# Two batches of attention prepared, and the first batch's maxima taken, among the expert loads before it

## The reference

```python
x = x + 0.5 * ffn(layernorm(x), gate_w, expert_bias, w1, w2, w3)
x = x + attention(layernorm(x), Wq, Wk, Wv, Wo)
x = x + 0.5 * ffn(layernorm(x), gate_w, expert_bias, w1, w2, w3)
```

## Time and profile before

| | us |
|---|---|
| median of 3 runs | 844.98 |
| the three runs | 844.72, 844.98, 851.7 |
| the profiled execution | 854.1 |
| its span, first to last instruction | 852.3 |

### The profile page before, as it was taken

One profiled execution on the slowest core, in us unless ns is written; L12 is line 12 of the kernel. 1 busy time (PEld: TensorE's weight loads), 2 busy tenths in 40 slices (PEclk: granted clock), 3 DMA queues, 4 the chain that ended last, 5 costly groups with the idle time before them and its releaser, 6 DMA issues.

```text
span 852.3 us, 14693 instructions
## 1 busy us (share of the span) xinstructions
PE 651.6 (76%) x4966; PEld 483.1 (57%) x4966; DVE 437.5 (51%) x1115; ACT 395.2 (46%) x926; POOL 302.3 (35%) x311
## 2 busy tenths in 40 slices
PE   4237999999987378887988999676798899889500
PEld 4236888888963134444544554335687788679400
DVE  3724572222345667977988888671457122123211
ACT  0333572433431157756867787583267234234200
POOL 4026543566313243034000000103654345554474
PEclk9999999999995569999989999865899889899855
DMA  6154795777826334244423432015379567567422
GB/s 227 37 182 108 220 265 171 221 204 208 241 88 194 106 99 133 89 131 139 132 88 120 126 107 90 2 57 165 102 216 253 158 187 205 162 194 220 132 77 62
DMA packets 114747, 126.03 MB, mean 148 GB/s; under 512 B 12464, under 2 KB 96944, under 8 KB 114416
## 3 DMA queue, kind: packets, MB, share of 16 engines
q1 hardware_dynamic: 88688, 98.05, 38.2%
q0 software_dynamic: 9088, 18.63, 9.0%
q10 hardware_dynamic: 16896, 8.39, 3.3%
HBM read 89.37 MB, written 35.39 MB: 146 GB/s over the span
## 4 chain that ended last, share of the span: by engine, by line
PE 51%; DVE 19%; issue 10%; ACT 7%; POOL 5%; DMA 3%; another core or an unknown queue 3%; SPq 1%; ACTq 0%; DVEq 0%; POOLq 0%
PE banks L624 10%; PE banks L602 7%; PE banks L607 7%; PE banks L612 7%; DVE mx L917 6%; PE banks L823 6%; POOL rows L541 3%; ACT PT L837 3%; PE banks L753 2%; PE banks L592 2%; PE banks L796 2%; PE banks L462 2%; PE banks L442 2%; ACT oT L890 1%
## 5 line engine op out<-in xcount | busy, mean ns | idle before, releaser
L521 POOL DMA_INDIRECT xe<-routed_rows,idx x156 | 151.7, 972 | 214.9 <-DMA routed_rows<-xn 77.0
L917 DVE TENSOR_REDUCE mx<-banks 128x2 f32<-128x512 f32 x256 | 163.0, 685 | 26.0 <-PE banks L798 20.0
L541 POOL DMA_INDIRECT rows<-slots_out,slot x128 | 123.2, 962 | 106.2 <-ACT PT L837 33.0
L837 ACT ACTIVATE PT<-banks 128x512 f32<-128x512 f32 x256 | 140.3, 602 | 43.3 <-PE banks L809 36.0
L675 DVE TENSOR_TENSOR hidT<-banks,act 96x256 f32<-96x256 f32 (+1 forms) x92 | 34.9, 380 | 237.4 <-ACT act L657 173.0
L624 PE MATMUL banks<-WR,hidT 128*128 128x128 f32 x936 | 121.1, 277 | 5.1 <-ACT ye L665 4.3
L624 PEld LDWEIGHTS banks<-WR,hidT 128*128 128x128 f32 x936 | 113.2, 193 | 8.6 <-issue 6.5
L602 PE MATMUL banks<-xeT,WR 128*128 128x256 f32 (+1 forms) x368 | 93.0, 377 | 22.0 <-issue 20.4
L492 POOL TENSOR_TENSOR rough<-var,half_power 128x16 f32<-128x16 f32 (+1 forms) x8 | 18.4, 2296 | 220.4 <-DVE var L258 220.4
L607 PE MATMUL banks<-xeT,WR 128*96 128x256 f32 (+1 forms) x368 | 89.2, 367 | 6.3 <-DVE hidT L675 6.3
L612 PE MATMUL banks<-xeT,WR 128*128 128x256 f32 (+1 forms) x368 | 87.2, 361 | 0.0
(11 more groups left out here) (155 smaller groups left out, 851.0 us busy)
## 6 DMA issues: line engine op xcount, KB each, us to landing
WR<-in_experts SPq DMA_DIRECT2D x92, 544.0 KB
stacks<-split SPq DMA_DIRECT2D x32, 384.0 KB
slots_out<-ye SPq DMA_DIRECT2D x156, 64.0 KB
routed_rows<-xn ACTq DMA_DIRECT2D x32, 256.0 KB
QS<-stacks SPq DMA_DIRECT2D x64, 112.0 KB
KS<-stacks SPq DMA_DIRECT2D x64, 112.0 KB
xe<-routed_rows,idx POOLq DMA_INDIRECT x156
rows<-in_xt SPq DMA_DIRECT2D x2, 1024.0 KB, 9.4
```

The costliest lines, as they stand in the source:

```text
L521: eng.indirect_dma_start(xe[:, i % XR, a, :], None, routed_rows[h], bass.IndirectOffsetOnAxis(ap=idx[h][:, tile:tile + 1], axis=0))\
L541: eng.indirect_dma_start(rows[:, k, t, :], None, slots_out[h], bass.IndirectOffsetOnAxis(ap=slot[h][:, k, t:t + 1], axis=0))\
L837: eng.activation(PT[:, u % 4, 1 - k].rearrange("p t n -> p (t n)"), PS[f % 3], ACT.Exp, scale=scale).then_inc(s_exp2, 1)
L917: eng.tensor_reduce(mx[:, :, e, pair], MAXIMA[f % 3][:, :].rearrange("p (q n) -> p q n", q=2), AX.X, ALU.max).then_inc(s_max, 1)
```

## The change

It has five parts.

1. `attention_*` begin at round -1. What rounds -3 and -2 did for batches 0 and 1, and all sixteen maxima of batch 0, is done by `prologue_*` as side steps of loads 30 to 45 (7 to 22 of half 1). They use bank PS[7] alone; maximum f waits for the reduction of f-1. On TensorE and ScalarE some steps stand in the middle of a load (`between`), behind the up products.
2. `split` is two tiles in turn. `split_high` waits for the writes of batch m-2.
3. Finishing is by chunks: chunk 0 in loads 7 to 9, ahead of the prologue; chunk 1 in loads 18 to 22; chunk 2 in round 0; chunk 3 in rounds 1 and 2.
4. GpSimd has a program of its own for network 1 (`first_gpsimd`): chunk 0's eight result gathers right after load 26, chunk 1's one by one, tiles for half 1 as they are used, and chunks 2 and 3 paced by the maxima.
5. The routing's five steps a load become tables (VECTOR, SCALAR, TENSOR), in both networks. By them the power's user comes at load 3 (was 1), the one-hot tables at loads 14 and 15 (were in one load), the rows `xn` in loads 9 to 18 (were 7 to 13), the inverse's products half at load 16, half at load 17 (were all at 14), and `idx` at load 18 (was 15).

```diff
-        split = sb("split", [P, 2, 3, SEQ], BF16)
+        split = [sb(f"split{w}", [P, 2, 3, SEQ], BF16) for w in range(2)]
...
@@ expert_sync, expert_tensor, expert_scalar
+                aside(sides, i)
...
-        def expert_tensor(eng, first, last, *sides):
+        def expert_tensor(eng, first, last, *sides, between=()):
...
                 if i < last:
                     up(i)
+                aside(between, i)
                 if i + 1 < last:
                     turn(i + 1)
                 if i > first:
                     down(i - 1)
                 aside(sides, i)
...
+        def split_high(eng, m, bank):
+
+            eng.wait_ge(s_qk, m + 1)
+            if m >= 2:
+                eng.wait_ge(s_wr[m % 2], 64 * (m // 2))
+            eng.copy(split[m % 2][:, :, 0, :], bank[:, :].rearrange("p (s n) -> p s n", s=2)).then_inc(s_hi, 1)
...
+        def maxima_bank(f):
+            return PS[7] if f < 2 * PAIRS else MAXIMA[f % 3]
+
+        def prologue_tensor(eng):
+
+            for m in range(2):
+                if m == 0:
+                    eng.wait_ge(s_wa, 64)
+                    eng.wait_ge(s_vzero, 14)
+                    eng.wait_ge(s_lgread, 2 * HALVES)
+                else:
+                    eng.wait_ge(s_ve, m)
+                eng.wait_ge(s_xa, 2 * (m + 1))
+                turn_normed(eng, m, PS[7])
+                yield
+                queries_keys(eng, m, PS[7])
+                yield
+                value_rows(eng, m, PS[7])
+                yield
+            eng.wait_ge(s_ve, 2)
+            for f in range(2 * PAIRS):
+                for _ in largest_scores(eng, (0, f // 2), f % 2):
+                    pass
+                yield
+
+        def prologue_scalar(eng):
+
+            for m in range(2):
+                copy_turned(eng, m, PS[7])
+                yield
+                split_high(eng, m, PS[7])
+                yield
+                split_middle(eng, m)
+                copy_values(eng, m, PS[7])
+                yield
+
+        def prologue_vector(eng):
+
+            normed_pair(eng, 0)
+            yield
+            for m in range(2):
+                if m == 0:
+                    normed_pair(eng, 1)
+                split_rest(eng, m, PS[7])
+                yield
+                split_low(eng, m)
+                yield
+            for f in range(2 * PAIRS):
+                largest(eng, f)
+                yield
+
+        def prologue_sync(eng):
+
+            split_out(eng, 0)
+            yield
+            stack(eng, 0, 0)
+            yield
+            split_out(eng, 1)
+            yield
+            stack(eng, 0, 1)
+            yield
+            for c in range(2):
+                stack(eng, 1, c)
+                yield
...
@@ attention_tensor, attention_scalar, attention_vector, attention_sync
-            for n in range(-3, BATCH + 1):
+            for n in range(-1, BATCH + 1):
...
@@ largest_scores
-            wait(eng, s_max, f - 2)
+            wait(eng, s_max, f if f < 2 * PAIRS else max(f - 2, 2 * PAIRS))
...
+        def first_gpsimd(eng):
+
+            ins = chained(gathers_in(eng, 0), gathers_in(eng, 1))
+            outs = gathers_out(eng, 0)
+            for _ in range(8):
+                next(ins)
+            for i in range(2 * NL):
+                wait(eng, s_xt, i + 1)
+                if i == 2:
+                    root_gpsimd(eng, 1, 1)
+                if i == NL + 9:
+                    root_gpsimd(eng, 2, 0, tiles_of_chunks(0))
+                if i < NL + 3:
+                    next(ins, None)
+                    next(ins, None)
+                elif i < NL + 5:
+                    for _ in range(KT // GC // 2):
+                        next(outs)
+                else:
+                    for _ in range(load_of(i)[2]):
+                        next(ins, None)
+                    if i % 3 != 2 and i < NL + 17:
+                        next(outs)
+                if i == 2 * NL - 1:
+                    root_gpsimd(eng, 3, 0, tiles_of_chunks(1))
+            for _ in ins:
+                pass
+            for n in range(KT // 2, KT):
+                wait(eng, s_max, n if n < 3 * KT // 4 else 2 * n - 3 * KT // 4)
+                next(outs)
+                if n == 3 * KT // 4 + 3:
+                    root_gpsimd(eng, 4, 0, tiles_of_chunks(2))
+            root_gpsimd(eng, 5, 0, tiles_of_chunks(3))
...
-            return lambda i: 5 if g * NL <= i < (g + 1) * NL else 0
+        VECTOR = (3, 3, 1, 2, 13, 3, 3, 3, 15, 3, 3, 3, 2, 1, 1, 1, 19, 0, 1)
+        SCALAR = (0, 0, 0, 0, 17, 0, 0, 0, 0, 24, 3, 4, 3, 3, 4, 3, 3, 4, 2)
+        TENSOR = (0, 0, 0, 0, 0, 0, 0, 0, 39, 0, 0, 0, 0, 0, 0, 0, 33, 2)
+
+        AHEAD_TENSOR = 10 * (0,) + (1, 1, 0, 0, 0) + 8 * (1,)
+        AHEAD_TENSOR_MID = 10 * (0,) + (1, 1, 1, 1, 0) + 8 * (1,)
+        AHEAD_SCALAR = 10 * (0,) + (1, 1, 0, 0)
+        AHEAD_SCALAR_MID = 10 * (0,) + (1, 1, 1, 1)
+        AHEAD_VECTOR = 7 * (0,) + (2, 2, 3, 1, 1, 1, 1, 0) + 8 * (2,)
+        FINISH_VECTOR = 18 * (0,) + (1, 1, 1, 1, 2)
...
-            expert_sync(sp, 0, HALVES * NL)
+            expert_sync(sp, 0, HALVES * NL, (prologue_sync(sp), in_loads(NL + 14, 6), -1))
...
-            attention_vector(dve, (finish_group(dve, 1), from_step(-4), PAIRS),
+            attention_vector(dve, (finish(dve, 4, 0, 2), lambda i: 2 * int(2 <= i <= 4), 5),
+                             (finish(dve, 5, 0, 3), from_step(PAIRS + 2), 2 * PAIRS + 5),
```

More of the change, by code:

```diff
@@ L638, in expert_tensor, with expert_scalar @@
                 aside(sides, i)
-        def expert_scalar(eng, first, last, *sides):
+        def expert_scalar(eng, first, last, *sides, between=()):
             def turned(i):
@@ L687, in maxima_of, with turn_normed, queries_keys @@
             m, pair = n + 1 + (u >= 3), (u + 5) % PAIRS
-            return (m, pair) if 0 <= m < BATCH else None
+            return (m, pair) if 1 <= m < BATCH else None
+        def turn_normed(eng, m, bank):
+            for i in range(2):
+                last = eng.transpose(bank[:, i * P:(i + 1) * P], xa[:, i, :], ident)
+            last.then_inc(s_at, 1)
+        def queries_keys(eng, m, bank):
+            eng.wait_ge(s_ate, m + 1)
+            for part, w in enumerate((WQ, WK)):
+                last = eng.matmul(bank[:, part * SEQ:(part + 1) * SEQ], w[:], xaT[:], start=True, stop=True)
+            last.then_inc(s_qk, 1)
@@ new lines, in value_rows, with copy_turned @@
+        def value_rows(eng, m, bank):
+            eng.wait_ge(s_res, m + 1)
+            for kt in range(2):
+                last = eng.matmul(bank[:, kt * P:(kt + 1) * P], xaT[:, kt * P:(kt + 1) * P], WV[:],
+                                  start=True, stop=True)
+            last.then_inc(s_v, 1)
+        def copy_turned(eng, m, bank):
+            eng.wait_ge(s_at, m + 1)
+            wait(eng, s_v, m)
+            eng.copy(xaT[:], bank[:, 0:SEQ]).then_inc(s_ate, 1)
+        def split_high(eng, m, bank):
[3 more added lines that the diff above has]
+            eng.copy(split[m % 2][:, :, 0, :], bank[:, :].rearrange("p (s n) -> p s n", s=2)).then_inc(s_hi, 1)
@@ new lines, in split_middle, with copy_values, split_rest @@
+        def split_middle(eng, m):
+            eng.wait_ge(s_res, m + 1)
+            eng.copy(split[m % 2][:, :, 1, :], resid[:, :, :]).then_inc(s_mid, 1)
+        def copy_values(eng, m, bank):
+            eng.wait_ge(s_v, m + 1)
+            wait(eng, s_av, PAIRS // 2 * (m - 3))
+            eng.copy(V1[m % 4][:, :, :, 0:HD],
+                     bank[:, 0:2 * P].rearrange("p (k a d) -> p k a d", k=2, d=HD)).then_inc(s_ve, 1)
+        def split_rest(eng, m, bank):
+            eng.wait_ge(s_hi, m + 1)
+            wait(eng, s_lo, m)
+            eng.tensor_tensor(resid[:], bank[:, :].rearrange("p (s n) -> p s n", s=2),
+                              split[m % 2][:, :, 0, :], ALU.subtract).then_inc(s_res, 1)
```

187 lines of the change are left out of this document (86 added, 101 removed).

## The result

The changed kernel takes 888.3 us as the median of four executions, one of them an outlier of 1267 us; the five others on record take 882.6 to 891.9. The kernel before takes 845.8 beside it. Without the outlier the ratio is 1.047 (95% interval 1.040 to 1.055): slower by 4.7%, where 2.7% less was forecast. The profiled execution of after spans 889.7 us, 37.4 more than the 852.3 of before.

| stage | before, us | after, us | difference |
|---|---|---|---|
| experts, first half | 101.0 | 104.8 | +3.8 |
| experts, second half | 87.7 | 120.0 | +32.3 |
| last down product to first scores | 44.9 | 10.6 | -34.3 |
| first to last scores | 271.4 | 295.6 | +24.2 |
| second network, first half | 110.1 | 108.1 | -1.9 |

A forecast was written before the change was run, and what follows sets the result against it. TensorE was taken to bound the second half's experts, and the 45 us before attention to be a serial chain. Terms of -32.4, +3, +9, +3, +3.6 and -9 sum to -22.8: 844.98 becomes 822 us, range 809 to 835.

The forecast's parts named there:

- Term 1: From the experts' end to attention's first scores: preparation and maxima move ahead, 44.9 us become 12.5, -32.4 us.
- Term 2: In attention's new start: gaps read as code loading may recur, 0 to 6.6 us, taken as +3 us.
- Terms 3 and 4: Second half's experts: TensorE's added products and waits, +9 us (8 to 15); added transfers delaying weights, +3 (0 to 8).
- Rival B: Second half's experts: transfers starve TensorE and its clock falls, +24 us, 846 us or 850 with the waits; chance 0.04.
- The prediction's own sign of being wrong: Three signs: gap to first scores over 25 us, experts grown by over 20, or loads beside the routing keeping their waits.
- Term 5: Attention rounds 0 and 1: chunks 2 and 3 are finished there, where VectorE is near its limit, +3.6 us.
- its sentence that nobody else waits for GpSimd's gathers: Attention: sixteen gathers wait on maxima as before, are combined later, and nobody else waits for them in between; no cost.
- Term 6: Expert loads beside the routing, both networks: tables end waits for hidT and the clock's fall, -9 us (-10.7 to -3).
- GpSimd starts its 39 gathers at load 19, not 16 … That just fits: Experts' second half: at 1.3 us each, 21 gathers and chunk 0's eight are issued by about load 30, in time for VectorE.

The follow-up runs named there:

- e11: Changed kernel with the old side steps, attention's outgoing gathers one at a time and placed anew, six incoming gathers ahead of each network; 813.5 us beside 849.0 (0.959).
- e12: Kernel before, without any part of the change, with the same calm gathers and placing as e11; 827.4 us (0.977).
- m4: Kernel before with three probes in attention: six powers, 12 gathers each after the last landing, 12 after the last but one; chip with 804.7 us for before.
- e13: e11 with the tables by load back in both networks, incoming gathers two or three a load behind the late index; 781.3 us beside 801.9 (0.974).
- e5: Changed kernel with old side steps, outgoing gathers spread, and batch 0's maxima moved behind the loads; 815.0 us beside 804.7 (1.016).
- e2: Kernel before with the tables by load alone, in both networks; 877.0 us beside 854.1 (1.027).
- e6: e2 with at most two incoming gathers a load behind the late index; 858.5 us beside 846.9 (1.016).

## Why the prediction was wrong

**Term 1, the start, -32.4:** right. 10.6 us instead of the forecast 12.5, in place of 44.9; e11 against e12 -36.4. On the chip of m4, where the old start took 36.9 us, it is 26.3 (e13 against m4): part of the old start was, it seems, the harm of 15 gathers beside it (266.8 to 285.2).

**Term 2, gaps read as code loading, +3:** the mechanism was wrong. The 6.58 us of "issue" and the 3.79 us of the unknown queue stand beside runs of 15 and 6 gathers: a maximum's products that had ended at 280.65 have their update at 288.11, and products that had ended at 308.94 and 310.27 from 313.5 to 313.7. The new start has no gap in which the engines stop together. The rule of the Trainium skill that the forecast set aside (Runtime: NRT & Kernel Launch, "Instruction fetch mechanics": mostly hidden) gave 0, and 0 was measured. This was the point at which the forecast could have been saved: the unknown queue was in the profile with 3%, and what GpSimd did at those moments was not looked up.

**Terms 3 and 4, +12 together:** the mechanism right, the size 3 to 4 us short: +15.8 (e11 against e12), +15.2 (e13, 99.0 us, against m4, 83.8). The parts: preparation and transfers +9.0 (e5, 92.8 us, against m4 on one chip), the sixteen maxima +6.2 (e13 against e5, on two chips without the harm), against the 3.5 to 5.1 and the waits forecast. Rival B falls: with the same transfers the clock over the half is 1.00 in e13 and 0.98 in e11. In the changed kernel it is 0.92, 0.80 in the 30 us behind the first stall. The prediction's own sign of being wrong came: the experts of this half grew by over 20 (+32.3). With the same products and transfers and the gathers paced it is 15.8 (e11).

**Term 5, +3.6:** near the mark for what it priced. The first three rounds, in which chunks 2 and 3 are now finished, are longer by 4.8 us (e11 against e12), 3.6 (e13 against m4) and 7.2 (e5 against m4). Attention as a whole is longer by 10.2 and 7.8 (the latter without the round that m4's probe lengthened); 5.4 and 5.5 of it are in the fifth round, where gathers that go one at a time, as in these variants, come too late for VectorE, and TensorE waits 4.9 us for VectorE's next maximum. In e11:

```profile
347.67 0.69 DVE L556 TENSOR_TENSOR rows<-rows 128x512 f32<-128x512 f32 x1 [4.65 <-DMA rows<-slots_out,slot]
```

But its sentence that nobody else waits for GpSimd's gathers was the second failed step: it counted who waits for them, not what their closeness holds up. The changed kernel loses 24.2 us in attention, 18.5 of it in the one round beside the 16 gathers that had piled up behind a late root.

**Term 6, the tables, -9:** here the forecast broke. What it said of the tables themselves held: TensorE's wait for hidT, 6.3 us before, is gone in after, e2 and e13, and it is 9.1 us in m4, which has the old steps on a chip without the harm. The rows of after and of m4:

```profile
L608 PE MATMUL banks<-xeT,WR 128*96 128x256 f32 (+1 forms) x368 | 91.2, 374 | 0.0
L609 PE MATMUL banks<-xeT,WR 128*96 128x256 f32 (+1 forms) x368 | 86.2, 358 | 9.1 <-DVE hidT L677 9.1
```

On the chips without the harm the first half is 8.0 us shorter with the tables (90.3 in e13 against 98.3 in m4) and the second network's first half 9.8 (90.0 against 99.8; 99.0 in e5), twice the forecast, though e13 also has its gathers placed otherwise. The inverse in two pieces of 2.52 us (after, at 133.66 and 138.91) leaves the granted clock at 1.00 from 130 to 151 us, where it was 0.89 from 125 to 140 around the one piece of before. On a chip with the harm, e2 shows +23 us. The failed step is "GpSimd starts its 39 gathers at load 19, not 16 … That just fits": it counted what the gathers cost GpSimd, 1.3 us each, and not what their closeness costs TensorE. Issued as fast as they will go, 17 and 19 of them in a row, they hold up its updates by up to 15.6 us, and the loads beside them take 10.7, 12.6 and 17.7 us.

The sum of -22.8 is near the 20.6 us of e13, but partly by errors that cancel: a start worth 6 us less there, tables worth 9 more, no gap (3), terms 3 to 5 dearer by 7. That it comes near is luck, and e13 is not the change that was forecast: its gathers are paced. What the unedited change does on such a chip wasn't run.

## What stays open

Why gathers hold up TensorE's updates, and why in six of eight groups of runs, each on one chip (845 to 854 us for before), and not in two (802 and 805), no trace shows. That it is the chip rests on one group for each; no chip is known to have run twice.

One rival was not tested: that the recording has a part in it. The traces of the two kinds of chip differ in what they hold. ScalarE makes 918 updates; the 17 traces with the harm hold 738 to 805 of them, the three without it hold all, and of the transfers' updates the first hold 6,847 to 7,402 and the others 12,169 to 12,510. So on the same chips on which TensorE's updates come late, the record loses many of all kinds. Every time given here comes with a span and a granted clock from such a record, so no execution is known to have run without it. Whether gathers in a row cost a kernel anything when nothing records it is open.

The tables with calm gathers were timed on a chip without the harm only; e6, with runs of ten and eight gathers left, doesn't settle what they give on the others.

## What to carry to other kernels

Moving a producer later costs more than its wait when an engine behind it must catch up: look at what runs without gaps afterwards, and pace it by a counter of the work it serves, or by each transfer's own landing. A share of "another core or an unknown queue" on a single core is a finding; look up what every engine did in those microseconds before you name a cause. And time a change on more than one chip: here the kernel before differs by 6% between chips, and the tables, 23 us dearer on one of them, seem to save time on another.

## What the runs showed of the hardware

- Gathers issued by GpSimd within 0.3 us of one another come with late semaphore updates of TensorE, by up to 15.6 us, on most of the chips here, as far as executions under recording show: 12 gathers cost 13 us, 4 cost 1.5, with 32 rows as with 128.
- In the same stretches the updates of ScalarE and VectorE come within 0.02 us of the end.
- 12 plain transfers issued by GpSimd in 6.5 us, and 17 us of powers on it, cost nothing. 10 gathers, each issued when the one before had landed, cost 0.4 us.
- In two of eight groups of runs there was none of it, with 26 gathers in a row beside a busy TensorE.
